# Maxima of attention scores: one head's scores plus the relu of a difference of two heads, in place of copies

## The chip, the cores and the metric

One core of a Trainium2 chip runs the whole program. The metric is the device time of one execution in microseconds (us), as the median of several runs. Names of engines in the views: PE is TensorE (matmuls), PEld its weight loads, ACT is ScalarE, DVE is VectorE, POOL is GpSimd, SP issues the DMAs (SPq is its queue of instructions).

## The reference

The block adds a cross attention and a quantised feed-forward network to x. What bears on this change is the attention, whose softmax is not over the keys: it runs over all heads and batches together, for each pair of a query and a key.

```python
B, S, D, H = (8, 512, 256, 16)        # DK = 16
scores = jnp.einsum('bqhd,bkhd->hbqk', q, k) / np.sqrt(DK)
attn = jax.nn.softmax(scores.reshape(H * B, S, S), axis=0).reshape(H, B, S, S)
out = jnp.einsum('hbqk,bkhd->bqhd', attn, v).reshape(B, S, H * DK)
```

So each of the 512 x 512 pairs needs the maximum of its 128 scores (16 heads x 8 batches) before the exponentials are taken.

## The kernel before, in words

Four stages follow one another, each in a block of its own whose end all engines wait for. `prepare` (0 to 127.6 us) normalises x, projects queries and keys, splits them into bf16 parts and writes these as rows of two stacks in HBM, `k_stack` and `q_stack`; it also makes the values (`vpad`) and the weights of the last stage. `maxima` (127.6 to 310.9 us) finds the maxima. `attend` computes the scores again, exponentials, sums and products with the values. `ffn` is the rest.

`maxima` takes the heads two at a time (a couple p, heads 2p and 2p+1). The queries of both heads lie in one tile `q_both`: one head's 64 rows (4 parts of 16) in partitions 0 to 63, the other's in 64 to 127. The keys of the even head lie in `k_even` with zeros in partitions 64 to 127, those of the odd head in `k_odd` with zeros in 0 to 63, so that a matmul with either tile gives one head's scores. A matmul makes 128 keys (a chunk kc of NC = 4) by 512 queries of one batch, in one bank of PSUM.

The work is cut into 64 groups: a head and two batches (LANES), 4 chunks of keys, so 8 matmuls that fill all eight banks of `ps_max`. Of a group, ACT copies chunks 0 to 2 to SBUF as bf16 (L697, 3 instructions of 1024 elements), DVE takes the larger of `high` and the copies in one instruction (L713, 3072 elements), and takes chunk 3 directly from PSUM (L708, 1024 elements). The order on an engine is the order of the code:

```python
nc.vector.tensor_tensor(high[:, COPIED, :], ps[:, COPIED, :], high[:, COPIED, :], ALU.max)
nc.vector.tensor_tensor(high[:, 0:COPIED, :], copies[:, g % RING], high[:, 0:COPIED, :], ALU.max)
```

At the end L717 folds the two lanes of `high` into `shift`, which `attend` subtracts from the scores (L890).

SP loads the tiles of a couple while the couple before it is worked on (`load_pair`, L109 to L121), then issues three copies of rows inside the stacks that `attend` needs (L64), and at the last couple the first 20 tiles of `attend` (L652, L653). The first couple's even keys and its queries are loaded inside `prepare` (`k_first`, `q_first`, in a piece of the arena `qs` that is free by then), ahead of the last unit's five writes to `q_stack` (L279). POOL ends `prepare` with two memsets: the lower half of `k_first` (L300) and the gaps of `vpad` (L302).

## Time and profile before

| | us |
|---|---|
| runs: median (lowest, highest) of 3 | 859.45 (859.14, 860.92) |
| the profiled execution: its own time | 859.72 |
| its span, first to last instruction | 857.6 |
| of it `maxima`, from L676's first start to the start of `attend` | 127.71 to 310.88 |

The profiled execution's time is its span and 2.1 us around it. Busy times in a view are unions: two instructions of an engine that overlap by their pipelines count once, so the mean of one times their number may be more than the busy time.

### The profile page before, as it was taken

To read this page: it belongs to the slowest core of one execution; us is meant where nothing else is said; L and a number is where in the kernel's file an instruction comes from. 1 tells how busy PE (TensorE), PEld (TensorE's weight loads), DVE (VectorE), ACT (ScalarE), POOL (GpSimd) and SP (SyncE) were. 2 spreads that over 40 slices of the span, in tenths; PEclk is the share of its full clock that TensorE was granted. 3 is DMA by queue.
4 is the path that set the end of the run, shared out by engine and by line. 5 is a ranking of instruction groups with operands and counts; after the bars stand their busy time and mean duration, and the time that the engine had idled before them with its cause. 6 is when DMAs were issued, how large, how long until landed. Compare 5 with 4: busy or idle time off the path is not lost. (4 is left out here: it accounts for less than half of the span.)

```text
span 857.6 us, 20062 instructions
## 1 busy us (share of the span) xinstructions
PE 745.7 (87%) x8150; PEld 448.8 (52%) x8150; DVE 757.3 (88%) x830; ACT 680.7 (79%) x1095; POOL 475.2 (55%) x225
## 2 busy tenths in 40 slices
PE   8898987777777768999999999999999899569977
PEld 6564461112212235767767666767667677425334
DVE  4799638999999979999999999999999995748957
ACT  3444549999999977988999899999999835759873
POOL 1233554000000013999999999999999996414500
PEclk9999999999999989999999999999999999879989
DMA  9897787766776635668867786768867793000014
GB/s 292 275 306 221 245 257 196 196 172 171 196 196 173 245 92 187 185 199 271 258 188 210 242 284 191 227 205 278 253 192 208 223 321 107 0 1 1 1 49 148
DMA packets 98154, 164.30 MB, mean 192 GB/s; under 512 B 9680, under 2 KB 37072, under 8 KB 97744
## 3 DMA queue, kind: packets, MB, share of 16 engines
q1 hardware_dynamic: 98064, 163.03, 63.3%
q8 instruction: 65, 1.06, 0.5%
q14 instruction: 25, 0.20, 0.1%
HBM read 133.63 MB, written 41.94 MB: 205 GB/s over the span
## 5 line engine op out<-in xcount | busy, mean ns | idle before, releaser
L1009 POOL TENSOR_TENSOR e<-e,recip 128x1792 f32<-128x1792 f32 (+3 forms) x128 | 368.1, 2913 | 25.8 <-DVE recip L1040 25.7
L961 ACT ACTIVATE e<-psY 128x512 f32<-128x512 f32 x512 | 296.1, 645 | 41.9 <-PE psY L894 39.0
L1027 DVE TENSOR_REDUCE partial<-e 128x128 f32<-128x2048 f32 (+1 forms) x85 | 284.2, 3360 | 11.8 <-ACT e L961 11.6
L894 PE MATMUL psY<-arena 128*128 128x128 bf16 x2048 | 200.5, 221 | 0.1
L894 PEld LDWEIGHTS psY<-arena 128*128 128x128 bf16 x2048 | 149.0, 98 | 73.8 <-issue 26.6
L697 ACT ACTIVATE copies<-ps_max 128x1024 bf16<-128x1024 f32 x189 | 175.6, 1090 | 0.0
L890 PE MATMUL psY<-shift,minus 128*128 128x512 bf16 x395 | 152.4, 386 | 11.8 <-PEq L633 5.5
L713 DVE TENSOR_TENSOR high<-copies,high 128x3072 bf16<-128x3072 bf16 x63 | 110.3, 1750 | 0.4 <-ACT copies L697 0.4
L1000 POOL MEMSET ones_w<- 96x128 bf16 x1 | 0.2, 206 | 172.6 <-POOLq L633 172.6
L910 PE MATMUL psX<-e,arena 128*32 128x128 f32 x2048 | 76.6, 290 | 2.6 <-DVE e L1020 2.6
L708 DVE TENSOR_TENSOR high<-ps_max,high 128x1024 bf16<-128x1024 f32 x63 | 76.8, 1219 | 1.5 <-PE ps_max L676 1.5
L1020 DVE TENSOR_TENSOR e<-e,psY 128x256 f32<-128x256 f32 (+3 forms) x128 | 76.4, 637 | 1.6
L296 POOL TENSOR_TENSOR parts<-rest,parts 128x512 bf16<-128x512 f32 x32 | 37.7, 1183 | 70.8 <-ACT parts L440 70.7
L967 ACT ACTIVATE psY<-shift 128x512 f32<-128x512 bf16 x117 | 74.2, 634 | 0.0
L910 PEld LDWEIGHTS psX<-e,arena 128*32 128x32 f32 x2048 | 58.5, 110 | 10.8 <-POOL e L1009 2.9
L890 PEld LDWEIGHTS psY<-shift,minus 128*128 128x128 bf16 x395 | 38.6, 98 | 25.0 <-DMA arena<-k_stack 8.0
L910 PE MATMUL acc_last<-e,arena 128*32 128x128 f32 x1024 | 38.2, 288 | 8.2 <-POOL e L1009 7.8
L676 PE MATMUL ps_max<-q_both,k_odd 128*128 128x512 bf16 x128 | 34.5, 382 | 10.9 <-DVE high L708 5.5
L676 PE MATMUL ps_max<-q_both,k_even 128*128 128x512 bf16 x128 | 34.2, 382 | 11.1 <-ACT copies L697 5.7
L676 PE MATMUL ps_max<-arena,k_odd 128*128 128x512 bf16 x128 | 34.0, 382 | 11.1 <-ACT copies L697 5.8
L676 PE MATMUL ps_max<-arena 128*128 128x512 bf16 x128 | 34.0, 382 | 10.8 <-ACT copies L697 4.7
L1434 POOL TENSOR_TENSOR arena<-up,sil 128x512 f32<-128x512 f32 x20 | 25.4, 1270 | 31.8 <-ACT up L1367 24.5
(173 smaller groups left out, 1015.9 us busy)
## 6 DMA issues: line engine op xcount, KB each, us to landing
arena<-k_stack SPq DMA_DIRECT2D x256, 256.0 KB, 3.3
arena<-q_stack SPq DMA_DIRECT2D x64, 256.0 KB, 4.2
k_stack<-parts SPq DMA_DIRECT2D x40, 256.0 KB, 3.7
q_stack<-parts SPq DMA_DIRECT2D x40, 256.0 KB, 3.6
arena<-in_x_dram SPq DMA_DIRECT2D x8, 1024.0 KB, 10.2
k_stack<-k_stack SPq DMA_DIRECT2D x12, 512.0 KB, 11.5
arena<-in_ctx_dram SPq DMA_DIRECT2D x4, 1024.0 KB, 6.5
arena<-q_stack SPq DMA_DIRECT2D x8, 512.0 KB, 8.0
```

The source lines that it names most:

```text
L676: last = nc.tensor.matmul(ps[:, kc, j * S:(j + 1) * S], k_head[:, kc, b * P:(b + 1) * P], q_both[p % 2].rearrange("p c (b q) -> p c b q", ...
L697: nc.scalar.activation(dst, ps[:, kc, :], ACT.Copy).then_inc(copied, 1)
L708: nc.vector.tensor_tensor(high[:, COPIED, :], ps[:, COPIED, :], high[:, COPIED, :], ALU.max).then_inc(direct, 1)
L713: nc.vector.tensor_tensor(high[:, 0:COPIED, :], copies[:, g % RING], high[:, 0:COPIED, :], ALU.max).then_inc(updated, 1)
L890: nc.tensor.matmul(bank[:], minus[:], shift_at(qc, kc).to_broadcast([P, HB, P]), start=True, stop=False, skip_group_check=True)
L894: last = nc.tensor.matmul(bank[:, j * P:(j + 1) * P], ks[:, i % KRING, b * P:(b + 1) * P], qs[:, h, b * P:(b + 1) * P], start=False, stop= ...
L910: last = nc.tensor.matmul(acc[pair // BANK_PAIRS][grp:grp + 32, col:col + P], vpad[:, kc, b, v_col:v_col + 32], e_at(p, z, z + 1), start=F ...
L961: nc.scalar.activation(e_at(p, half * HB, (half + 1) * HB).rearrange("p q z i -> p z q i"), ps[n % SCORES][:].rearrange("p (z q i) -> p z ...
L967: nc.scalar.activation(ps[(n - 1) % SCORES][:].rearrange("p (b q) -> p b q", q=P), shift_at((p + 1) // CHUNK, (p + 1) % CHUNK // PAIRS).to ...
L1009: nc.gpsimd.tensor_tensor(part, part, by_pairs(recip[:, r % 2, :], share), ALU.mult).then_inc(pool_scaled, 1)
L1020: nc.vector.tensor_tensor(part, part, by_pairs(recip_v[:, (r % 2) * P:(r % 2 + 1) * P], BLOCKS - share), ALU.mult).then_inc(dve_scaled, 1)
L1027: nc.vector.tensor_reduce(partial[:, :, k, :], e[:, t:t + n].rearrange("p t q z i -> p q i t z"), AX.XY, ALU.add).then_inc(sum_done, 1)
```

## The change

For key chunks 0 to 2 the larger of two heads' scores is made before any merging, as odd + relu(even - odd). A group is now both heads of a couple and one batch; there are again 64.

- The tile `k_mix` takes the place of `k_even`: even keys in partitions 0 to 63 and, for chunks 0 to 2, the odd head's keys times -1 in 64 to 127. A matmul with it gives even minus odd. POOL makes the negated half from `k_odd` after its load (TENSOR_SCALAR, 64 x 3072, once a couple). Chunk 3 of that half stays zero.
- TensorE, per group: `differences` (3 matmuls to `ps_x`), `plain` (2 matmuls of chunk 3, one a head, to `ps_c`), and for the group before it `larger`: per chunk one matmul of the odd keys and one of the identity `plus` with `gain`, added in the same bank of `ps_y`. 11 in place of 8.
- ScalarE, per group: relu of `ps_x` to `gain` as bf16 (1024 and 512 elements) and a copy of `ps_c` (1024).
- VectorE, per group: the larger of `ps_y` and `shift` (512 and 1024 elements, from PSUM) and of the copies and `high` (1024, bf16 in SBUF). The fold at the end has only chunk 3.
- The odd keys of the first couple are now loaded in `prepare` too, ahead of the other three loads; POOL zeroes their half and makes the first negated half there, ahead of the memset of `vpad`.

```diff
-    if even is not None:
-        sp.dma_start(even[0:HALF], rows(k_stack, 2 * p)).then_inc(loaded, 16)
-    if both is not None:
-        for j in range(2):
-            sp.dma_start(both[j * HALF:(j + 1) * HALF], rows(q_stack, 2 * p + j)).then_inc(loaded, 16)
-    if odd is not None:
-        sp.dma_start(odd[HALF:P], rows(k_stack, 2 * p + 1)).then_inc(loaded, 16)
+    sp.dma_start(odd[HALF:P], rows(k_stack, 2 * p + 1)).then_inc(odd_loaded, 16)
+    sp.dma_start(mix[0:HALF], rows(k_stack, 2 * p)).then_inc(loaded, 16)
+    for j in range(2):
+        sp.dma_start(both[j * HALF:(j + 1) * HALF], rows(q_stack, 2 * p + j)).then_inc(loaded, 16)
...
-                pool.memset(keep["k_first"][HALF:P], 0.0).then_inc(s["k_zeroed"], 1)
-                pool.wait_ge(s["k_zeroed"], 1)
+                pool.memset(keep["k_first"][HALF:P, NC - 1, :], 0.0).then_inc(s["k_zeroed"], 1)
+                pool.memset(keep["k_odd_first"][0:HALF], 0.0).then_inc(s["k_zeroed"], 1)
+                pool.wait_ge(s["k_zeroed"], 2)
+                pool.wait_ge(keep["odd_first_loaded"], 16)
+                nc.gpsimd.tensor_scalar(keep["k_first"][HALF:P, 0:NC - 1, :], keep["k_odd_first"][HALF:P, 0:NC - 1, :],
+                                        -1.0, None, ALU.mult).then_inc(keep["first_negated"], 1)
+                pool.wait_ge(keep["first_negated"], 1)
...
+                def differences(g):
+                    p = g // B
+                    if g % B == 0:
+                        pe.wait_ge(couple_loaded[p % 2], 16 * 3 * (p // 2 + 1))
+                        pe.wait_ge(negated[p % 2], p // 2 + 1)
...
+                    for kc in range(MIXED):
+                        if g:
+                            pe.wait_ge(gained, 2 * (g - 1) + (2 if kc == MIXED - 1 else 1))
+                        nc.tensor.matmul(ps_x[:, kc, :], keys(k_mix, g, kc), queries(g), start=True, stop=True
+                                         ).then_inc(x_scored, 1)
+                def plain(g):
+                    if g:
+                        pe.wait_ge(c_copied, g)
+                    for j, tile in enumerate((k_mix, k_odd)):
+                        last = nc.tensor.matmul(ps_c[:, j, :], keys(tile, g, MIXED), queries(g), start=True, stop=True)
+                    last.then_inc(c_scored, 1)
+                def larger(g):
...
+                    for kc in range(MIXED):
+                        if g:
+                            pe.wait_ge(y_merged, 2 * (g - 1) + (1 if kc == 0 else 2))
+                        nc.tensor.matmul(ps_y[:, kc, :], keys(k_odd, g, kc), queries(g), start=True, stop=False)
+                        pe.wait_ge(gained, 2 * g + (2 if kc == MIXED - 1 else 1))
+                        nc.tensor.matmul(ps_y[:, kc, :], plus[:], gain[:, g % RING, kc, :], start=False, stop=True
+                                         ).then_inc(y_scored, 1)
+                for g in range(GROUPS):
+                    differences(g)
+                    plain(g)
+                    if g:
+                        larger(g - 1)
+                larger(GROUPS - 1)
...
+                for g in range(GROUPS):
+                    if g >= RING:
+                        act.wait_ge(y_scored, MIXED * (g - RING + 1))
+                    for k0, k1 in ((0, MIXED - 1), (MIXED - 1, MIXED)):
+                        act.wait_ge(x_scored, MIXED * g + k1)
+                        nc.scalar.activation(gain[:, g % RING, k0:k1, :], ps_x[:, k0:k1, :], ACT.Relu
+                                             ).then_inc(gained, 1)
+                    act.wait_ge(c_scored, g + 1)
+                    if g > RING:
+                        act.wait_ge(c_merged, g - RING)
+                    nc.scalar.activation(copies[:, g % RING, :] if g else high[:], ps_c[:].rearrange("p j q -> p (j q)"),
+                                         ACT.Copy).then_inc(c_copied, 1)
...
+                for g in range(GROUPS):
+                    for n, (k0, k1) in enumerate(((0, 1), (1, MIXED))):
+                        dve.wait_ge(y_scored, MIXED * g + k1)
+                        if g:
+                            dve.wait_ge(y_merged, 2 * (g - 1) + n + 1)
+                            nc.vector.tensor_tensor(shift[:, k0:k1, :], ps_y[:, k0:k1, :], shift[:, k0:k1, :], ALU.max
+                                                    ).then_inc(y_merged, 1)
...
+                    if g:
+                        dve.wait_ge(c_copied, g + 1)
+                        if g > 1:
+                            dve.wait_ge(c_merged, g - 1)
+                        nc.vector.tensor_tensor(high[:], copies[:, g % RING, :], high[:], ALU.max).then_inc(c_merged, 1)
```

TensorE in the middle of `maxima`, a group before:

```order
L676 MATMUL ps_max<-arena 128x512 [waits max_copied]
L676 MATMUL ps_max<-arena 128x512
L676 MATMUL ps_max<-arena 128x512 [waits max_copied]
L676 MATMUL ps_max<-arena 128x512
L676 MATMUL ps_max<-arena 128x512 [waits max_copied]
L676 MATMUL ps_max<-arena 128x512
L676 MATMUL ps_max<-arena 128x512 [waits max_direct]
L676 MATMUL ps_max<-arena 128x512
```

and a group now (`ps_x` differences, `ps_c` plain scores of chunk 3, `ps_y` the larger ones of the group before):

```order
L680 MATMUL ps_x<-arena 128x512 [waits max_gained] x3
L688 MATMUL ps_c<-arena 128x512 [waits max_c_copied]
L688 MATMUL ps_c<-arena 128x512
L698 MATMUL ps_y<-arena 128x512 [waits max_y_merged]
L700 MATMUL ps_y<-gain,plus 128x512 [waits max_gained]
L698 MATMUL ps_y<-arena 128x512 [waits max_y_merged]
L700 MATMUL ps_y<-gain,plus 128x512 [waits max_gained]
L698 MATMUL ps_y<-arena 128x512 [waits max_y_merged]
L700 MATMUL ps_y<-gain,plus 128x512 [waits max_gained]
```

The two plain matmuls stand between the differences of a group and the six matmuls of the group before it, so TensorE passes to those six only when ScalarE has copied the last `ps_c`.

POOL at the end of `prepare`, before:

```order
L296 TENSOR_TENSOR parts<-rest,parts 128x512 [waits part2_ready] x32
L300 MEMSET arena 64x4096 [waits part3_ready,transposed]
L302 MEMSET arena 128x256x16 [waits k_zeroed]
L229 UNCONDITIONAL_BRANCH
```

and now:

```order
L293 TENSOR_TENSOR parts<-rest,parts 128x512 [waits part2_ready] x32
L297 MEMSET arena 64x1024 [waits part3_ready,transposed]
L298 MEMSET arena 64x4096
L301 TENSOR_SCALAR arena<-arena 64x3072 [waits odd_first_loaded,k_zeroed]
L304 MEMSET arena 128x256x16 [waits first_negated]
L226 UNCONDITIONAL_BRANCH
```

The memset of `vpad` (the last row but one) is now queued behind a load and a multiplication.

SP's only change of order ahead of `maxima` is one more load (the odd keys) in front of the first couple's other three; the last five writes to `q_stack` follow them as before.

## Rows read from the trace of the kernel before

**Rows 1.** The page: the span
```profile
span 857.6 us, 20062 instructions
```

**Rows 2.** Busy time by stretch: PE, PEld, DVE, ACT, POOL (busy us, instructions, granted clock, DMA share, GB/s)
```profile
150.00:200.00 50.00, 38.84 (x145) 9.60 (x144) 50.00 (x36) 50.00 (x55) 0.00 (x0) 1.00 0.69 180
```

**Rows 3.** Groups by line in the stretch 125 to 311 us
```profile
L697 ACT ACTIVATE copies<-ps_max 128x1024 bf16<-128x1024 f32 x189 | 175.6, 1090 | 0.0
...
L713 DVE TENSOR_TENSOR high<-copies,high 128x3072 bf16<-128x3072 bf16 x63 | 110.3, 1750 | 0.4 <-ACT copies L697 0.4
...
L708 DVE TENSOR_TENSOR high<-ps_max,high 128x1024 bf16<-128x1024 f32 x63 | 76.8, 1219 | 1.5 <-PE ps_max L676 1.5
```

**Rows 4.** Timeline inside the stage (start, us, instruction, idle before and releaser)
```profile
198.39 1.75 DVE L713 TENSOR_TENSOR high<-copies,high 128x3072 bf16<-128x3072 bf16 x1
...
198.53 1.47 PE L676 MATMUL ps_max<-q_both,k_even 128*128 128x512 bf16 x6 [0.45 <-DVE high L708]
...
200.05 1.22 DVE L708 TENSOR_TENSOR high<-ps_max,high 128x1024 bf16<-128x1024 f32 x1
...
201.19 1.75 DVE L713 TENSOR_TENSOR high<-copies,high 128x3072 bf16<-128x3072 bf16 x1
```

**Rows 5.** Timeline, the stage's first instructions
```profile
127.71 2.32 PE L676 MATMUL ps_max<-arena 128*128 128x512 bf16 x10 [0.72 <-PEq L229]
...
128.34 2.85 ACT L697 ACTIVATE high<-ps_max 128x1024 bf16<-128x1024 f32 x3 [0.93 <-PE ps_max L676]
```

**Rows 6.** Timeline, a run of 512-column activations of the next stage
```profile
312.12 0.61 ACT L961 ACTIVATE e<-psY 128x512 f32<-128x512 f32 x1 [3.98 <-PE psY L894]
...
314.59 10.70 ACT L961 ACTIVATE e<-psY 128x512 f32<-128x512 f32 x21 [0.16 <-PE psY L894]
```

**Rows 7.** Tile ps_max, durations min/median/max of a matmul
```profile
L676 PE MATMUL ps_max<-q_both,k_even x128: 376/379/391, 148.8 to 294.0; 128*128 128x512 bf16 x128
```

**Rows 8.** Timeline, end of the stage and start of the next
```profile
309.37 1.22 DVE L717 TENSOR_TENSOR shift<-high 128x2048 bf16<-128x2048 bf16 x1
...
310.88 0.21 POOL L1000 MEMSET ones_w<- 96x128 bf16 x1 [172.57 <-POOLq L633]
```

**Rows 9.** Timeline, end of the preparing stage
```profile
111.78 3.51 POOL L300 MEMSET arena<- 64x4096 bf16 x1
...
113.78 0.63 SPq L116 DMA_DIRECT2D arena<-k_stack  x1
...
115.35 3.52 POOL L302 MEMSET arena<- 128x4096 f32 x1
...
115.88 3.31 SPq L279 DMA_DIRECT2D q_stack<-parts  x5
...
127.03 0.38 ACT L483 ACTIVATE wd_row<-psT 128x256 f32<-128x256 f32 x1 [0.86 <-PE psT L407]
```

**Rows 10.** SP's own waits, and the load of 113.78 us to its landing
```profile
SPq L229 <- DMA q_stack<-parts: 7.9, 1, 7.9
...
arena<-k_stack SPq DMA_DIRECT2D x1, 512.0 KB, 5.9
```

**Rows 11.** Busy time by stretch, around the stage's two ends
```profile
110.00:112.00 2.00, 2.00 (x6) 1.62 (x6) 0.25 (x1) 0.79 (x3) 1.87 (x3) 0.50 0.97 299
...
118.00:120.00 2.00, 2.00 (x14) 1.70 (x13) 0.75 (x3) 0.65 (x3) 0.86 (x1) 1.00 1.07 207
...
298.00:301.00 3.00, 2.07 (x8) 0.57 (x8) 3.00 (x4) 3.00 (x5) 0.00 (x0) 1.00 0.18 67
```

**Rows 12.** Groups by line of POOL
```profile
L296 POOL TENSOR_TENSOR parts<-rest,parts 128x512 bf16<-128x512 f32 x32 | 37.7, 1183 | 70.8 <-ACT parts L440 70.7
...
L992 POOL CAST bo_parts<-arena 96x256 bf16<-96x256 f32 x1 | 0.4, 393 | 2.8 <-DMA arena<-in_L_xattn_bo_dram 2.8
```

**Rows 13.** Tile k_odd, issue to landing; timeline of SP at the stage's end
```profile
DMA to landing us min/median/max: 5.6/10.3/11.9
...
283.23 0.35 SPq L652 DMA_DIRECT2D arena<-k_stack  x1
```

More of the change, by code:

```diff
@@ L602, in maxima @@
 def maxima(nc, sem, k_stack, q_stack, keep):
[L611 to L614 removed]
+    shift, plus = keep["shift"], keep["plus"]
     RING = 2
[L616 removed]
+    MIXED = NC - 1
     COUPLES = H // 2
+    GROUPS = COUPLES * B
     with ExitStack() as es:
@@ L620, in head_tile @@
             return es.enter_context(nc.sbuf_tensor(name, [P, NC, CT], BF16))
-        k_even = [keep["k_first"], head_tile("k_even1")]
-        k_odd = [head_tile("k_odd0"), head_tile("k_odd1")]
+        k_mix = [keep["k_first"], head_tile("k_mix1")]
+        k_odd = [keep["k_odd_first"], head_tile("k_odd1")]
         q_both = [keep["q_first"], head_tile("q_both1")]
-        copies = es.enter_context(nc.sbuf_tensor("copies", [P, RING, COPIED, LANES * S], BF16))
+        gain = es.enter_context(nc.sbuf_tensor("gain", [P, RING, MIXED, S], BF16))
+        copies = es.enter_context(nc.sbuf_tensor("copies", [P, RING, 2 * S], BF16))
+        high = es.enter_context(nc.sbuf_tensor("high", [P, 2 * S], BF16))
         spare = es.enter_context(nc.sbuf_tensor("spare_exp", [P, 1], F32))
-        high = es.enter_context(nc.sbuf_tensor("high", [P, NC, LANES * S], BF16))
-        ps = es.enter_context(nc.psum_tensor("ps_max", [P, NC, LANES * S], F32))
-        even_loaded, odd_loaded = ([sem(f"{n}{i}") for i in range(2)] for n in ("even_loaded", "odd_loaded"))
-        scored, copied, direct, updated, tiles_zeroed, folded = (
-            sem(n) for n in ("max_scored", "max_copied", "max_direct", "max_updated", "tiles_zeroed", "max_folded"))
+        ps_x = es.enter_context(nc.psum_tensor("ps_x", [P, MIXED, S], F32))
+        ps_y = es.enter_context(nc.psum_tensor("ps_y", [P, MIXED, S], F32))
+        ps_c = es.enter_context(nc.psum_tensor("ps_c", [P, 2, S], F32))
+        odd_loaded, couple_loaded, negated = ([s, sem(n)] for s, n in (
+            (keep["odd_first_loaded"], "odd_loaded1"), (keep["first_loaded"], "couple_loaded1"),
+            (keep["first_negated"], "negated1")))
+        x_scored, c_scored, y_scored, gained, c_copied, y_merged, c_merged, tiles_zeroed, folded = (
+            sem("max_" + n) for n in ("x_scored", "c_scored", "y_scored", "gained", "c_copied", "y_merged", "c_merged",
+                                      "tiles_zeroed", "folded"))
         with nc.Block() as block:
@@ L635, in _ @@
             def _(sp):
[L636 removed]
+                for p in range(1, COUPLES):
                     if p >= 2:
[L638 to L644 removed]
+                        sp.wait_ge(y_scored, MIXED * B * (p - 1))
+                    load_couple(sp, p, k_stack, q_stack, k_mix[p % 2], k_odd[p % 2], q_both[p % 2],
+                                odd_loaded[p % 2], couple_loaded[p % 2])
+                    for what in STACK_COPIES[COPIES_A_COUPLE * (p - 1):COPIES_A_COUPLE * p]:
+                        copy_rows(sp, k_stack, q_stack, what, keep["k_copied"], keep["q_copied"])
+                for what in STACK_COPIES[COPIES_A_COUPLE * (COUPLES - 1):]:
+                    copy_rows(sp, k_stack, q_stack, what, keep["k_copied"], keep["q_copied"])
                 for c in range(NC):
@@ new lines, in queries, with keys @@
+                def queries(g):
+                    return q_both[g // B % 2].rearrange("p c (b q) -> p c b q", q=P)[:, :, g % B, :]
+                def keys(tile, g, kc, rows=slice(0, P)):
+                    return tile[g // B % 2][rows, kc, g % B * P:(g % B + 1) * P]
+                def differences(g):
[3 more added lines that the diff above has]
+                        pe.wait_ge(negated[p % 2], p // 2 + 1)
+                    if p == 1 and g % B == 0:
+                        pe.wait_ge(tiles_zeroed, 2)
+                    for kc in range(MIXED):
[3 more added lines that the diff above has]
+                                         ).then_inc(x_scored, 1)
@@ L681, in _ @@
+                for g in range(GROUPS):
[4 more added lines that the diff above has]
+                larger(GROUPS - 1)
             @block.gpsimd
             def _(pool):
-                zeros = (k_odd[0], slice(0, HALF)), (k_even[1], slice(HALF, P)), (k_odd[1], slice(0, HALF))
-                for n, (tile, rows) in enumerate(zeros):
-                    if n:
-                        pool.wait_ge(tiles_zeroed, n)
-                    pool.memset(tile[rows], 0.0).then_inc(tiles_zeroed, 1)
+                pool.memset(k_mix[1][HALF:P, MIXED, :], 0.0).then_inc(tiles_zeroed, 1)
@@ new lines, in _ @@
+                pool.memset(k_odd[1][0:HALF], 0.0).then_inc(tiles_zeroed, 1)
+                pool.wait_ge(tiles_zeroed, 2)
+                for p in range(1, COUPLES):
+                    pool.wait_ge(odd_loaded[p % 2], 16 * (p // 2 + 1))
+                    nc.gpsimd.tensor_scalar(k_mix[p % 2][HALF:P, 0:MIXED, :], k_odd[p % 2][HALF:P, 0:MIXED, :],
+                                            -1.0, None, ALU.mult).then_inc(negated[p % 2], 1)
+                    pool.wait_ge(negated[p % 2], p // 2 + 1)
```

83 lines of the change are left out of this document (17 added, 66 removed).

## The prediction

> **What bounds the kernel now.** The page gives the span, 857.6 us [rows 1]; the stage of the maxima is 183 us of it, from the first matmul at 127.71 [rows 5] to the next stage's start at 310.88 [rows 8]. The busy time by stretch comes next: in the middle of the stage DVE and ACT are busy all the time, PE for 38.84 of 50 us, at a granted clock of 1.00 [rows 2]. The groups by line tell which of the two is the limit: DVE's two instructions hardly ever wait (0.4 and 1.5 us in the whole stage) [rows 3]. In the timeline L713 begins at 198.39 and again at 201.19, so a group takes **2.80 us**: 1.66 us from L713 to L708, 1.14 from L708 to L713 [rows 4]. DVE is the bound. ACT is close behind: from (2.85 - 1.02) / 2, a 1024-element copy begins 0.915 us after the one before it [rows 5], so three take 2.75. PE begins a 512-column matmul every (2.32 - 0.38) / 9 = 0.216 us [rows 5, 7]: eight take 1.73. A change pays here if DVE and ACT both get less to do and PE's slack pays for it; 64 groups make each 0.1 us of a group worth 6.4 us.
>
> **Work per group after the change.** DVE's start-to-start times are 1.14 us for 1024 elements from PSUM and 1.66 for 3072 in SBUF [rows 4]. If the fixed part is the same in both, at twice the rate per element in the second (1.66 = f + 1536 u, 1.14 = f + 1024 u), then u = 1.02 ns and f = 0.10 us. The merge of 512 elements from PSUM is then 0.62, that of 1024 from PSUM 1.14, that of 1024 in SBUF 0.62: **2.38** at most; with the 0.60 that a u of 1.04 gives it is 2.34. ACT: two of 1024 at 0.915, and one of 512 at (10.70 - 0.61) / 20 = 0.505 [rows 5, 6], **2.34**. I take relu at the price of a copy of the same size; no relu is in these rows. PE: 11 x 0.216 = **2.38**. All three engines would be full within two per cent, so the handing over decides.
>
> **The ring.** ps_x, ps_c and ps_y fill PSUM once, without a second buffer, and PE works in program order. The longest way round passes through PE and ACT and takes two groups: plain matmuls of group g (2 x 0.216), six of the group before (6 x 0.216), first two differences of g+1 until they can be read (0.216 + 0.379 [rows 7] + 0.04 until ACT begins: the second matmul of a pair begins 0.216 after 127.71 and ACT at 128.34 [rows 5]), then ACT's relu 0.915, small relu 0.505 and the whole of the copy, 1.02, and 0.05 until PE begins the plain matmuls of g+2. 0.432 + 1.296 + 0.635 + 0.915 + 0.505 + 1.02 + 0.05 = 4.85 us, 2.43 a group. DVE's ring is shorter: last merge from PSUM 1.22, 0.05, four matmuls 0.65 + 0.38 + 0.04, in all 2.34. I take **2.43**.
>
> The whole stage: the first plain matmul starts after three differences (0.65), the 64th 63 x 2.43 = 153.1 later; then 0.43 for it and its partner and 0.43 for the first chunk of group 62, 1.07 for its other two, DVE's merge of them 1.27, four matmuls of group 63 1.07, and on DVE 1.14 + 0.62 and a fold of 512 elements to its end 0.69 (0.62, and the 0.08 by which 1.22 is above 1.14): 160.5 us from the first matmul to the end of the fold. Before, this was 309.37 + 1.22 - 127.71 = 182.9 [rows 5, 8]. **-22.4 us.**
>
> **The end of the preparing stage.** Two engines close it nearly together: ACT with L483 at 127.41 [rows 9], and SP, whose last writes to q_stack, issued until 119.2, land 7.9 us after it began to wait, at 127.1 [rows 9, 10]. The new load of odd keys, 512 KB, goes into the same queue ahead of these writes, when the DMA engines are full (share 1.07 at 118 to 120, 207 GB/s) and move up to 300 GB/s elsewhere [rows 11]: it pushes the writes back by 1.7 to 2.5 us. I take 2.0: SP ends at 129.1, ACT's 127.4 is no longer the last, **+1.7 us**. POOL's chain: memsets at 3.51 us for 4096 elements [rows 9], so 0.9 and 3.5 from 111.8 to 116.2; the odd keys, issued at 113.78 like the load that landed in 5.9 [rows 9, 10], are there at 119.7; the multiplication of 3072 elements is priced between a memset (2.6 us) and a two-input instruction (1183 ns for 512, 7.1 us) [rows 9, 12]; nearest is the cast, one input, 393 ns for 256 [rows 12], of which some 0.1 us is fixed: 3.5. Then the vpad memset, 3.52: POOL ends at 126.8, between 125.8 and 130.4. I take it as hidden under SP's 129.1; it costs up to 1.3 us at its upper end.
>
> **What is hidden.** The seven later multiplications (3.5 us each) and the loads of a couple have 7 groups' time, 17 us, since loads are released one group into the couple before; keys land in at most 11.9 us [rows 13], and 11.9 + 3.5 is below 17. If they came late it would be by under 2 us a couple even at 7.1. The next stage's 20 first tiles are issued from 283.23 and over by 298 [rows 11, 13], 15 us; they will be released some 20 us ahead of the stage's end and stay hidden by 5. The matmuls beyond eight a group are in the ring above.
>
> **Sum.** 859.72 (the profiled execution: span 857.6 and 2.1 around it) - 22.4 + 1.7 = 839.0. That execution is 0.3 above the median of the runs, so **838.7 us** against 859.45.
>
> **A rule against it.** While the chip grants the stage a clock of 1.00, PE is idle in short pieces for 22% of it [rows 2]; so short pauses between groups have not lowered the clock. The Trainium skill (TensorE: Matmul & The Clock Gate, "A second HAM failure mode: psum-queue depth-cycling") says that a kernel which goes round the PSUM banks with such small idle pieces sees its clock swing between the two levels. This trace disagrees with it, with its 1.00 over 50 us; by the rule the time would be that of rival 4.
>
> **Rivals.**
> 1. *The handing over costs more.* Engines full to 96 or 98% have nothing to catch up with: each step that comes 0.05 us late in a ring of some six steps adds 0.15 a group. At 2.6 us a group the saving is 11 us less: 850. For it: the three prices are equal within two per cent, and relu and the identity matmuls are in no row. Against: instructions of a kind hardly vary here (376 to 391 ns [rows 7]). 0.17.
> 2. *The start is later.* POOL's chain or the load takes its upper price, and PE, idle for 2.4 us and more before the stage, starts at the lower clock: PE got 0.50 after such a pause at 110 to 112 [rows 11], and some 3 us of it would cost half of that. +2 to +4: 842. 0.10.
> 3. **Slower than before**: *PE stands still behind ps_c.* The plain matmuls of a group wait for ACT's copy of the last one, which ACT does after both relus. If ACT is late, relus and matmuls no longer overlap but take turns: three differences until readable 0.85, two relus and copy to the end 2.44, two handovers 0.1 make 3.4 a group, 64 x 0.97 = 62 us more than in the sum: 901. It decides from 2.75 us a group on, where 64 groups and the later start reach the old 182.9. Against it: while ACT copies, PE has six other matmuls that wait for nothing of that group, and the two-group ring above closes at 2.43. 0.03.
> 4. **Slower**: *the clock falls in the stage.* At the lower level, 1.2 GHz, a matmul takes 0.43, a group 4.75: 64 x 2.32 = 148 us more, 987; already a seventh of the stage at it takes the gain away. Against it: PE will be busier than in the stretch that had 1.00 [rows 2]. 0.03.
> 5. *POOL holds DVE up.* The merge in SBUF has two inputs there, and POOL multiplies beside it for 7 x 3.5 = 25 us; if that quarter of DVE's work stood still as long, 6 us: 845. Rows show only memsets beside L713, which has such inputs, and its mean is 1750 all the same [rows 3]. The GPSIMD Engine Reference of the Trainium skill (its table of the engine's properties) says that the two share SBUF interfaces when a DVE instruction has two SBUF inputs; no multiplication here shows it. 0.04.
>
> **How the numbers follow.** The forecast has 0.63: 832 to 846, from a group of 2.38 (PE's and DVE's own work, -3), a start that loses nothing (-2) and a start of the next stage at full clock after a shorter pause of PE (-1.5), to 2.50 (+4.5) and a start at upper prices (+3). To hold the time 8 times in 10 the range takes rivals 1, 2 and 5: **832 to 852**. A measurement can tell about 0.2%, 1.7 us, from no change. Faster by more: forecast, 1, 2 and 5, less what lies beyond 2.70 us a group: 0.91. Within: 0.03. Slower: 0.06.
>
> **What would show it.** Right: in the new timeline a group takes 2.38 to 2.5 us, DVE and ACT at 93% or more and PE above 93% of the stage, with waits of PE for the copy of ps_c among its longest; SP ends the preparing stage at 128.5 to 130; relus 1.02 and 0.61 us, merges 1.22 and 0.69. Wrong: relus or the identity matmul of another price; a granted clock under 1.00 inside the stage; PE waiting for DMA or POOL at the first group of a couple; a group above 2.6 us with no engine full.

## The result and the profile after

The change makes the kernel slower: **890.67 us** (median of 4 runs, 889.51 to 891.96) against 859.3 for the kernel before beside it, a ratio of 1.0376 [1.035, 1.0402]. Forecast were 838.7 us, 832 to 852: wrong in direction and outside the range. The profiled execution took 889.51 us, with a span of 887.6 against 857.6 [rows 1]. The 30.0 us between the spans lie so, by each stage's first matmul:

| us | before | after | forecast | measured |
|---|---|---|---|---|
| `prepare`, until the first matmul of `maxima` | 127.71 | 134.63 | +1.7 | **+6.9** |
| `maxima`, until the first matmul of `attend` | 183.35 | 211.56 | -22.4 | **+28.2** |
| the rest | 546.54 | 541.41 | 0 | -5.1 |

The stage has the loss. Its groups by line (125 to 347 us):

```profile
L744 DVE TENSOR_TENSOR shift<-ps_y,shift 128x1024 bf16<-128x1024 f32 x63 | 77.0, 1223 | 9.8 <-PE ps_y L700 7.5
L752 DVE TENSOR_TENSOR high<-copies,high 128x1024 bf16<-128x1024 bf16 x63 | 76.8, 1218 | 0.0
...
L728 ACT ACTIVATE gain<-ps_x 128x1024 bf16<-128x1024 f32 x64 | 65.5, 1024 | 24.9 <-PE ps_x L680 22.8
...
L744 DVE TENSOR_TENSOR shift<-ps_y,shift 128x512 bf16<-128x512 f32 x63 | 43.1, 684 | 7.0 <-PE ps_y L700 6.0 <-remote 1.0
...
L728 ACT ACTIVATE gain<-ps_x 128x512 bf16<-128x512 f32 x64 | 38.0, 593 | 0.0
L717 POOL TENSOR_SCALAR k_mix<-k_odd 64x3072 bf16<-64x3072 bf16 x4 | 31.8, 7948 | 59.8 <-DMA k_odd<-k_stack 59.8
```

Merges from PSUM (1223, 684 ns) and relus (1024, 593 ns) have the prices of the forecast. Two rows do not: L752, forecast at half the price of a PSUM merge, has a mean of 1218 ns; and POOL's multiplication takes 7948 ns where 3.5 us were taken. The durations of L752 (min/median/max) say that the mean hides two kinds:

```profile
L752 DVE TENSOR_TENSOR high<-copies,high x63: 674/681/6323, 144.7 to 344.6; 128x1024 bf16<-128x1024 bf16 x63
```

56 of them take 0.68 us; seven take 2.44, 5.94, 6.24, 5.84, 5.93, 5.96 and 6.32. Each of the seven begins inside one of POOL's seven multiplications and ends 1.18 us before its record does. One in the timeline:

```profile
165.37 7.95 POOL L717 TENSOR_SCALAR arena<-arena 64x3072 bf16<-64x3072 bf16 x1 [17.04 <-DMA arena<-k_stack]
...
166.19 5.94 DVE L752 TENSOR_TENSOR high<-copies,high 128x1024 bf16<-128x1024 bf16 x1
...
167.23 0.81 PE L680 MATMUL ps_x<-q_both,k_mix 128*128 128x512 bf16 x3
172.06 1.81 DVE L744 TENSOR_TENSOR shift<-ps_y,shift 128x512 bf16<-128x512 f32 x2
172.23 1.02 ACT L733 ACTIVATE copies<-ps_c 128x1024 bf16<-128x1024 f32 x1 [5.17 <-DVE high L752]
173.15 1.51 ACT L728 ACTIVATE gain<-ps_x 128x1024 bf16<-128x1024 f32 x2
```

The merge ends at 172.13, POOL's record at 173.32. In between everybody stands: ACT's copy waits for the tile that the merge reads, PE's plain matmuls wait for ACT's copy. TensorE after it:

```profile
173.31 0.61 PE L688 MATMUL ps_c<-q_both,k_mix 128*128 128x512 bf16 x1 [5.27 <-ACT copies L733]
173.71 0.63 PE L688 MATMUL ps_c<-q_both,k_odd 128*128 128x512 bf16 x1
174.13 0.63 PE L698 MATMUL ps_y<-q_both,k_odd 128*128 128x512 bf16 x1
...
177.96 0.38 PE L688 MATMUL ps_c<-q_both,k_mix 128*128 128x512 bf16 x1
178.18 0.38 PE L688 MATMUL ps_c<-q_both,k_odd 128*128 128x512 bf16 x1
```

For over 4 us a matmul begins every 0.43 us, then every 0.22 again. Busy time by stretch (length, then PE, PEld, DVE, ACT, POOL, granted clock, DMA share, GB/s) has the same: full clock, the stall, the lower level of 1.2 GHz for most of 7 us, full clock.

```profile
160.00:166.00 6.00, 5.99 (x29) 2.32 (x28) 5.75 (x7) 5.78 (x8) 0.63 (x1) 1.00 0.72 169
166.00:172.00 6.00, 1.99 (x9) 0.66 (x8) 6.00 (x2) 1.06 (x2) 6.00 (x1) 0.93 1.30 345
172.00:179.00 7.00, 5.69 (x16) 2.13 (x17) 4.98 (x7) 4.50 (x6) 1.32 (x1) 0.58 0.39 163
179.00:186.00 7.00, 6.99 (x32) 2.72 (x31) 6.67 (x9) 6.79 (x9) 0.00 (x0) 1.00 0.00 1
```

From one L752 to the next, undisturbed groups take 2.38 and 2.56 us in turn, **2.47**; around a multiplication come groups of 7.6, 4.3 and 3.0 us. The first is the stall (5.1 above 2.47), the other two the slow matmuls (2.3).

The end of `prepare`, and how SP waited there:

```profile
122.55 8.00 POOL L301 TENSOR_SCALAR arena<-arena 64x3072 bf16<-64x3072 bf16 x1 [3.38 <-DMA arena<-k_stack]
...
128.29 0.38 ACT L485 ACTIVATE wd_row<-psT 128x256 f32<-128x256 f32 x1 [0.86 <-PE psT L409]
130.61 3.52 POOL L304 MEMSET arena<- 128x4096 f32 x1
134.44 0.61 SPq L115 DMA_DIRECT2D k_odd<-k_stack  x1
```

```profile
SPq L226 <- DMA q_stack<-parts: 9.6, 1, 9.6
...
SPq L226 <- PEq L226: 2.3, 1, 2.3
```

ACT's last copy begins 1.3 us later than before [rows 9]; SP's writes land 3.6 us after that; POOL ends last, at 134.13, and SP stands 2.3 us at the block's end for it. This profile is at the late end of a spread: in seven others with the same `prepare` (from the experiments below) the first matmul of the stage comes at 130.5 to 133.5 us. The `prepare` of the kernel before has it at 127.7, 127.3 and 128.4 in three profiles.

### The profile page after: what moved, and what is told of

Same layout as the page of the kernel before. It is cut to its first block and busy times, and to the rows that moved or that the text cites. A ratio compares the mean times of both kernels' runs of the same rounds, so it can differ in the third digit from the quotient of the medians.

```text
span 887.6 us, 20617 instructions
## 1 busy us (share of the span) xinstructions
PE 780.8 (88%) x8307; PEld 477.8 (54%) x8342; DVE 768.7 (87%) x894; ACT 657.1 (74%) x1095; POOL 533.7 (60%) x233
## 5 line engine op out<-in xcount | busy, mean ns | idle before, releaser
L744 DVE TENSOR_TENSOR shift<-ps_y,shift 128x512 bf16<-128x512 f32 x126 | 118.6, 954 | 16.8 <-PE ps_y L700 13.4
L728 ACT ACTIVATE gain<-ps_x 128x1024 bf16<-128x1024 f32 (+1 forms) x128 | 96.8, 808 | 24.9 <-PE ps_x L680 22.8
L733 ACT ACTIVATE copies<-ps_c 128x1024 bf16<-128x1024 f32 x63 | 64.6, 1025 | 33.3 <-DVE high L752 33.3
L752 DVE TENSOR_TENSOR high<-copies,high 128x1024 bf16<-128x1024 bf16 x63 | 76.8, 1218 | 0.0
L700 PE MATMUL ps_y<-gain,plus 128*128 128x512 bf16 x179 | 72.2, 404 | 0.0
L717 POOL TENSOR_SCALAR k_mix<-k_odd 64x3072 bf16<-64x3072 bf16 x4 | 31.8, 7948 | 59.8 <-DMA k_odd<-k_stack 59.8
L717 POOL TENSOR_SCALAR arena<-arena 64x3072 bf16<-64x3072 bf16 x3 | 23.8, 7946 | 55.4 <-DMA arena<-k_stack 55.4
L345 PE MATMUL psP<-xT,wq_p 128*128 128x512 f32 x64 | 35.8, 692 | 5.7 <-DVE xT L521 3.4
```

The source lines that it names most:

```text
L700: nc.tensor.matmul(ps_y[:, kc, :], plus[:], gain[:, g % RING, kc, :], start=False, stop=True).then_inc(y_scored, 1)
L728: nc.scalar.activation(gain[:, g % RING, k0:k1, :], ps_x[:, k0:k1, :], ACT.Relu).then_inc(gained, 1)
L744: nc.vector.tensor_tensor(shift[:, k0:k1, :], ps_y[:, k0:k1, :], shift[:, k0:k1, :], ALU.max).then_inc(y_merged, 1)
L752: nc.vector.tensor_tensor(high[:], copies[:, g % RING, :], high[:], ALU.max).then_inc(c_merged, 1)
```

## Experiments

The theory from these rows: POOL's multiplication holds up the DVE instruction whose two inputs are both in SBUF, for nearly its whole length, and the stall then costs TensorE its clock. Rivals: the extra load, the clock by itself, some lateness of the key tiles. In the cuts of code, "..." marks lines left out. Every kernel ran beside the kernel before (858 to 859 us); "stage" is from the first matmul to the end of the fold, 182.9 before and 211.1 after.

**Without the seven multiplications.** Left out are POOL's multiplications in `maxima`; the negated keys of couples 1 to 7 are missing and the maxima with them. All loads stay.

```diff
-                        pe.wait_ge(negated[p % 2], p // 2 + 1)
+                        if p == 0:
+                            pe.wait_ge(negated[0], 1)
...
-                pool.memset(k_mix[1][HALF:P, MIXED, :], 0.0).then_inc(tiles_zeroed, 1)
+                pool.memset(k_mix[1][HALF:P], 0.0).then_inc(tiles_zeroed, 1)
...
-                for p in range(1, COUPLES):
...
-                    nc.gpsimd.tensor_scalar(k_mix[p % 2][HALF:P, 0:MIXED, :], k_odd[p % 2][HALF:P, 0:MIXED, :],
-                                            -1.0, None, ALU.mult).then_inc(negated[p % 2], 1)
```

> POOL's seven multiplications of the stage are left out (the negated half of k_mix is zeros or the first couple's, so the maxima are not the reference's); the one in the preparing stage stays. Theory (VectorE's merge with both inputs in SBUF stands still while GpSimd multiplies): every L752 takes 0.68 us, a group 2.47 us throughout, the stage about 163 us from first matmul to the end of the fold in place of 211.1, the clock 1.00 in it, total 890.7 - 48 = 843. Rival A (the stalls come from the loads of the next couple, which land in the same stretch and stay in): L752 still takes 6 us seven times, total 885 or more. Rival B (the clock falls by itself from PE's short pauses): stretches at 0.50 stay, total above 860.

Measured: 842.69 us, ratio 0.9806 [0.9776, 0.9835]. Durations of the SBUF merge, and busy time by stretch:

```profile
L748 DVE TENSOR_TENSOR high<-copies,high x63: 681/681/682, 140.4 to 293.4; 128x1024 bf16<-128x1024 bf16 x63
```

```profile
150.00:200.00 50.00, 49.80 (x224) 19.58 (x222) 48.56 (x62) 48.72 (x61) 0.00 (x0) 1.00 0.67 180
```

No long merge, no low clock, a stage of 163.5 us: 47.6 less than after. The loads are all still there, so they are not the cause.

**VectorE multiplies.** The seven multiplications move to DVE, after the fifth group of the couple before.

```diff
...
+                    if g % B == B - 4 and g // B + 1 < COUPLES:
+                        p = g // B + 1
+                        dve.wait_ge(odd_loaded[p % 2], 16 * (p // 2 + 1))
+                        nc.vector.tensor_scalar(k_mix[p % 2][HALF:P, 0:MIXED, :], k_odd[p % 2][HALF:P, 0:MIXED, :],
+                                                -1.0, None, ALU.mult).then_inc(negated[p % 2], 1)
```

> The seven multiplications of the stage are done by VectorE, between the merges of the fourth and the fifth group of the couple before; the first stays on GpSimd in the preparing stage. Theory: no merge above 0.7 us; a multiplication of 64 x 3072 bf16 takes VectorE about 0.9 us, at most 3.3 at one element a cycle, so the stage is 163 + 7 x 0.9 = 169 us at most, total 845 to 850. Rival (it is the reading and writing of k tiles next to the loads that is slow, whichever engine does it): the multiplication takes several us on VectorE too, total above 870.

Measured: 848.13 us, ratio 0.9865 [0.9819, 0.9912], stage 169.4. The whole work of 7.95 us on POOL takes DVE 0.96:

```profile
170.25 0.96 DVE L751 TENSOR_SCALAR arena<-arena 64x3072 bf16<-64x3072 bf16 x1
```

The result is a complete kernel that is 1.3% faster than before: it pays for the multiplications openly, with seven groups of 3.44 us.

**POOL in six pieces.** The same work on POOL, each multiplication cut into six of 512 columns.

```diff
...
-                    nc.gpsimd.tensor_scalar(k_mix[p % 2][HALF:P, 0:MIXED, :], k_odd[p % 2][HALF:P, 0:MIXED, :],
-                                            -1.0, None, ALU.mult).then_inc(negated[p % 2], 1)
+                    for c in range(MIXED):
+                        for half in range(2):
+                            x = slice(half * CT // 2, (half + 1) * CT // 2)
+                            nc.gpsimd.tensor_scalar(k_mix[p % 2][HALF:P, c, x], k_odd[p % 2][HALF:P, c, x],
+                                                    -1.0, None, ALU.mult).then_inc(negated[p % 2], 1)
...
```

> GpSimd multiplies in six instructions of 64 x 512 in place of one of 64 x 3072. Theory 1 (VectorE waits for the end of the instruction that GpSimd is in): L752 takes at most 0.7 + 1.4 us, and each couple meets two or three such waits of about 1 us: the stage is 165 to 175 us, total 845 to 858. Theory 2 (the port stays with GpSimd over its queued instructions): as the change, L752 of 6 us, total 890.

Measured: 843.24 us, ratio 0.9818 [0.9785, 0.9852], stage 164.4: a little better than the first theory's 845 to 858.

```profile
L721 POOL TENSOR_SCALAR k_mix<-k_odd x24: 1486/1487/1944, 137.0 to 267.0; 64x512 bf16<-64x512 bf16 x24
```

```profile
L756 DVE TENSOR_TENSOR high<-copies,high x63: 675/681/1045, 140.0 to 293.8; 128x1024 bf16<-128x1024 bf16 x63
```

POOL works longer in sum (6 x 1.49 = 8.9 us), yet the longest merge is 1.05 us and no group is over 2.7: nearly all 47 us are back. It is the length of one POOL instruction that costs, not POOL's work in sum.

**POOL in three pieces.** As before, with 1024 columns each.

> GpSimd's multiplication in three instructions of 64 x 1024 (2.75 us each by the slope between 1.49 us for 512 and 7.95 for 3072). Theory (a merge waits for what is left of the instruction that GpSimd is in, up to about 0.5 us for 512 and 6.1 for 3072 from its start, on a line 1.6 for 1024): merges up to 2.2 us, 1 to 2 of them a couple, stage 170 us at most, total 844 to 850. Rival (below some length GpSimd's instructions never hold VectorE, whatever is left of them): as in six, 843.

Measured: 848.43 us, ratio 0.9887 [0.9854, 0.9919], stage 169.7.

```profile
204.06 8.46 POOL L719 TENSOR_SCALAR arena<-arena 64x1024 bf16<-64x1024 bf16 x3 [12.11 <-DMA arena<-k_stack]
...
207.29 1.19 DVE L754 TENSOR_TENSOR high<-copies,high 128x1024 bf16<-128x1024 bf16 x1
```

The price of a piece (2.77 us) and the total came as expected, the longest merge did not: 1.19 us, where 2.2 were expected, and two or three of them a couple. Every merge that is held up ends 1.19 us before the record of the piece (208.48 against 209.67, the end of the second of the three), as in the kernel after (172.13 against 173.32). If it then works for its undisturbed 0.68, it starts to work about 1.87 us before the end of POOL's record. By this a piece of 2.77 us keeps a merge from working for its first 0.9 us, the whole one of 7.95 for 6.1. In the run with six pieces merges end 0.33 us before the record, so they start 1.02 before it: a piece of 1.49 us holds a merge for its first 0.47 alone.

**The kernel before, with such a multiplication.** POOL multiplies a tile of its own, which nobody reads, once in each of seven couples.

```diff
...
+                pool.memset(busy[HALF:P], 1.0).then_inc(busied, 1)
+                for p in range(1, COUPLES):
+                    pool.wait_ge(odd_loaded[p % 2], 16 * (p // 2 + 1))
+                    for i in range(1):
+                        pool.wait_ge(busied, 1 * (p - 1) + i + 1)
+                        nc.gpsimd.tensor_scalar(busy[HALF:P], busy[HALF:P], -1.0, None, ALU.mult).then_inc(busied, 1)
```

> The kernel before, with a multiplication of 64 x 3072 bf16 by GpSimd on a tile of its own once in each of seven couples; nothing waits for it. Theory: L713, whose inputs both lie in SBUF, meets each of them once and takes up to 8 us there; L708 keeps 1.22; about 7 x (8 - 1) us less what ScalarE and TensorE catch up (nothing, VectorE is the bound): total 859 + 45 to 55 = 904 to 914. Rival (the stall is of the new kernel's own chain, not of the port): 859, L713 at 1.75 throughout.

Measured: 897.09 us, ratio 1.0446 [1.0412, 1.0479], stage 221.1; 904 to 914 were expected, with 7 us for each meeting, and the long merges are 4.9 to 6.0 us above their usual 1.74.

```profile
L716 DVE TENSOR_TENSOR high<-ps_max,high x63: 1209/1211/1225, 131.9 to 344.2; 128x1024 bf16<-128x1024 f32 x63
L721 DVE TENSOR_TENSOR high<-copies,high x63: 1740/1742/7735, 133.5 to 345.3; 128x3072 bf16<-128x3072 bf16 x63
```

No data, tile or semaphore links the two engines here, and still seven of the SBUF merges take 6.6 to 7.7 us, while no merge from PSUM is touched. Here the stage's 38.2 us are the stalls alone: the seven long merges are 37.9 us over 7 x 1.742. All seven end 0.12 us before POOL's record. With their own 1.74 us of work they start 1.86 before it, as the short merges above do. It goes the other way too: two of the multiplications began while a merge was at work, and it was they that got longer, 8.63 and 9.45 us in place of 7.95:

```profile
194.49 1.74 DVE L721 TENSOR_TENSOR high<-copies,high 128x3072 bf16<-128x3072 bf16 x1
194.59 9.45 POOL L695 TENSOR_SCALAR busy<-busy 64x3072 bf16<-64x3072 bf16 x1 [20.64 <-DMA k_odd<-k_stack]
```

The clock falls here too:

```profile
174.88 1.74 DVE L721 TENSOR_TENSOR high<-copies,high 128x3072 bf16<-128x3072 bf16 x1
175.02 4.58 PE L678 MATMUL ps_max<-q_both,k_odd 128*128 128x512 bf16 x14 [5.54 <-DVE high L716]
...
177.69 1.74 DVE L721 TENSOR_TENSOR high<-copies,high 128x3072 bf16<-128x3072 bf16 x1
```

```profile
174.00:181.00 7.00, 5.57 (x18) 1.86 (x19) 7.00 (x6) 6.71 (x8) 0.00 (x0) 0.74 0.01 2
```

but the group after the stall lasts 2.81 us as always, although the granted clock is 0.74 in this stretch: with eight matmuls a group PE has the slack for it, with eleven it has none.

**The kernel before, with memsets instead.** Three memsets of 64 x 3072 in place of each multiplication (`pool.memset(busy[HALF:P], 1.0)`).

> The kernel before, with three memsets of 64 x 3072 bf16 by GpSimd (2.65 us each, 8 us) where the earlier run had one multiplication, once in each of seven couples. Theory (it is GpSimd's reading of SBUF that keeps VectorE's second input out; a memset reads nothing): L713 stays at 1.75 us, total 859. Rival (any long use of SBUF by GpSimd, writing too, holds VectorE): L713 of several us seven times, total 880 to 897.

Measured: 860.9 us in one run, against 858.08 (855.26 to 862.71) for the kernel before; stage 183.3.

```profile
L721 DVE TENSOR_TENSOR high<-copies,high x63: 1744/1744/1759, 135.1 to 308.7; 128x3072 bf16<-128x3072 bf16 x63
```

```profile
L695 POOL MEMSET busy<- 64x3072 bf16 x21 | 55.7, 2652 | 85.4 <-DMA k_odd<-k_stack 84.6
```

POOL was busy for 55.7 us beside the merges, as in the kernel after, and held up none, though multiplications of nearly the length of one of these memsets (2.77 us, above) did. So the memsets that stood beside L713 before [rows 3] could not have shown the cost. A memset reads nothing, and that the reading makes the difference fits this run; no run shows that it is the reading and no other difference of the two.

**Chunk 3 read from PSUM.** In the kernel after, DVE takes the larger of `ps_c` and `high` directly, first in its group; ACT's copy goes. No DVE instruction of a group then has two SBUF inputs.

```diff
...
-                        pe.wait_ge(c_copied, g)
+                        pe.wait_ge(c_merged, g)
...
+                    dve.wait_ge(c_scored, g + 1)
...
+                        nc.vector.tensor_tensor(high[:], plain_v, high[:], ALU.max).then_inc(c_merged, 1)
...
```

> GpSimd multiplies as in the change, in one instruction; VectorE reads chunk 3 straight from PSUM (one input in SBUF in place of two) and ScalarE does not copy it. Theory (only a VectorE instruction with both tensor inputs in SBUF stands still beside GpSimd's multiplication): no merge above 1.3 us although GpSimd is at work for the same 8 us seven times; VectorE's own work is 1.14 + 0.62 + 1.14 = 2.90 us a group, so 64 x 2.90 + 5 = 190 us of stage, total 866 to 872, and no group beyond 3.1 us. Rival (any VectorE instruction stands still beside GpSimd): merges of 6 us as in the change, total 910 or more.

Measured: 961.06 us, ratio 1.1201 [1.1159, 1.1244]. The total missed by 90 us, through a ring that I had built myself:

```profile
PEld ps_c L688 <- DVE high L739: 126.2, 55, 2.3
PE ps_c L688 <- DVE high L739: 99.1, 55, 1.8
...
DVE shift L746 <- PE ps_y L700: 71.6, 110, 1.1
```

PE's plain matmuls wait for DVE's merge of `ps_c`, and DVE's next merges wait for the matmuls that PE issues behind them. What it was made for came out all the same: with seven POOL multiplications of 7.95 us beside them, no merge got longer; the one that now reads `ps_c` has one length:

```profile
L739 DVE TENSOR_TENSOR high<-ps_c,high x63: 1215/1215/1215, 140.0 to 409.7; 128x1024 bf16<-128x1024 f32 x63
```

PE stood still for 1.8 us in each group of 4.35 here, 62 times, and the granted clock stayed at 1.00.

**Plain matmuls last.** Six pieces, and PE's `larger(g - 1)` ahead of `plain(g)`. It tests the ring through `ps_c` from which 2.43 us a group were forecast.

```diff
...
                     differences(g)
-                    plain(g)
                     if g:
                         larger(g - 1)
+                    plain(g)
...
```

> The run with GpSimd's multiplication in six instructions; TensorE does the six matmuls of the group before ahead of the two plain ones, so that it no longer stands before ScalarE's copy of ps_c with six ready matmuls behind. Theory (the two-group ring through ps_c and ScalarE makes 2.47 us a group, TensorE's own work is 2.38): groups of 2.38, the stage 164.4 - 64 x 0.09 = 158.6 us, total 837 to 838. Rival (TensorE's own work and waiting of any kind make the 2.47): no change, 843; or, if VectorE's ring is now the longer, slower.

Measured: 840.15 us, ratio 0.9792 [0.9758, 0.9825], stage 159.2 where 158.6 were expected, an undisturbed group 2.37 to 2.38.

```profile
150.00:200.00 50.00, 49.97 (x231) 20.90 (x229) 50.00 (x63) 49.55 (x64) 20.15 (x13) 1.00 0.68 180
```

PE, DVE and ACT are full: the ring was the limit, and without it the engines' own work is, 11 x 0.216 = 2.38. The same kernel once more, beside the ones that follow:

> The run with the two plain matmuls last once more, as the measure for the next two on the same chip: 840, stage 159.2 us. Theory and rival expect the same.

838.54 us, ratio 0.977 [0.974, 0.98]. The two profiles of this one kernel differ around the stage: it starts 6.5 us after ACT's last copy in the first and 4.5 in the second, and what follows the stage takes 545.7 and 542.8 us. Differences of 2 or 3 us outside the stage are within this spread.

**The first couple's multiplication on VectorE.** It stands in `prepare`, behind the last but one value tile, once on the kernel in six pieces and once on the one with the plain matmuls last.

```diff
-                nc.gpsimd.tensor_scalar(keep["k_first"][HALF:P, 0:NC - 1, :], keep["k_odd_first"][HALF:P, 0:NC - 1, :],
-                                        -1.0, None, ALU.mult).then_inc(keep["first_negated"], 1)
...
+                    if v == NC * B // 2 - 2:
+                        dve.wait_ge(keep["odd_first_loaded"], 16)
+                        nc.vector.tensor_scalar(keep["k_first"][HALF:P, 0:NC - 1, :],
+                                                keep["k_odd_first"][HALF:P, 0:NC - 1, :],
+                                                -1.0, None, ALU.mult).then_inc(keep["first_negated"], 1)
```

> The run with GpSimd's multiplication in six instructions, and the first couple's multiplication in the preparing stage done by VectorE before its last addition of values. Theory (GpSimd's 8 us and its memset behind them close the preparing stage): the stage begins at SP's arrival, 1.5 to 2.5 us sooner after ScalarE's last copy, total 841 to 842 against 843.2. Rival (the stage's start is set by the landing of q_stack alone): unchanged, 843.

Measured: 844.03 us, ratio 0.9833 [0.9805, 0.9861]; from ACT's last copy to the stage 4.1 us instead of 6.5, yet the total does not differ from the six pieces, which is what the rival expected. SP's wait for POOL at the block's end fell from 2.1 to 0.2 us: POOL no longer closes `prepare`, but no gain in the total is shown.

> The run with the two plain matmuls last, and the first couple's multiplication done by VectorE in the preparing stage. Theory (GpSimd's chain closes the preparing stage 2.3 to 2.4 us after SP's arrival): the stage starts 4.1 us after the start of ScalarE's last copy in place of 6.5, total 2 us less than the run it is compared with, 838. Rival (what is won there is lost in the next stages, whose loads or clock decide): no difference.

Measured: **836.86 us**, ratio 0.974 [0.9707, 0.9774], the lowest of all. The stage starts 4.95 us after ACT's last copy, where 4.1 were expected; without the edit it was 6.5 and 4.5. Against the same kernel without this edit on the same chip (838.54) the 1.7 us lie within the intervals, so a gain is not shown here either.

**The load of the odd keys behind the writes.** On the kernel with plain matmuls last, the first odd load is issued after the last five writes to `q_stack`, and DVE multiplies at the stage's start.

> The run with the two plain matmuls last, the first couple's odd keys loaded behind the last writes to q_stack in place of ahead of them, and multiplied by VectorE at the stage's very start. Theory (the load ahead of the writes delays SP's arrival by 3.5 to 4.5 us): SP arrives about when it did before the change, within 1 us of ScalarE's last copy, the first difference waits for load and multiplication instead, 2 to 3 us into the stage: total 1 to 2 us below the run with VectorE's multiplication in the preparing stage, 836 to 837. Rival (the load costs the same wherever it stands): equal to that run.

Measured: 840.29 us, ratio 0.9783 [0.9754, 0.9813]; 836 to 837 were expected. SP now arrives 1.4 us after ACT's last copy began, against 2.2 to 4.8 in the other kernels of the change. From the last issue of the writes to their landing it is 8.2 us, against 9.6 to 10.2 with the load ahead (7.9 in the kernel before [rows 10]): the load does push the writes back. But what was gained is lost at once:

```profile
130.58 3.50 POOL L714 MEMSET k_odd<- 64x4096 bf16 x1
...
131.28 3.62 DVE L744 TENSOR_SCALAR arena<-arena 64x3072 bf16<-64x3072 bf16 x1 [4.36 <-DMA arena<-k_stack]
```

The multiplication that takes DVE 0.96 us elsewhere takes 3.62 here, beside a POOL memset, and ends 0.82 us after it; the first matmul waits for the multiplication.

## Why the prediction was wrong

**Right.** The prices per instruction: matmuls every 0.216 us, relu at the price of a copy (1.02 and 0.59), merges of 1.22 and 0.68. The ring through `ps_c`: 2.43 forecast, 2.47 measured in undisturbed groups, and gone (2.38) once the plain matmuls came last. Without the seven multiplications the stage took 163.5 us; 160.5 were forecast, and 64 x 0.04 = 2.6 of the difference is what a group took beyond 2.43. The loads of a couple and the first tiles of the next stage stayed hidden. Rivals 1 and 3 did not come about. While the stage runs undisturbed, with short waits of PE for `ps_c`, the clock stays at the 1.00 of the stretches above. Inside the stage it fell in six of the seven stalls, in which PE stood still for 5.0 to 5.5 us. The rule of the Trainium skill that was weighed (TensorE: Matmul & The Clock Gate, "A second HAM failure mode: psum-queue depth-cycling") was not borne out by these stretches.

**The step that failed** is the one under "What is hidden", on the seven later multiplications of POOL. They did come in time, each done 9.0 to 11.5 us before the first matmul that needs it, but what they do to others was put at nothing in the sum. Rival 5 named this mechanism and got 6 us and a chance of 0.04; it cost 47.6 us. The Trainium skill's GPSIMD Engine Reference (Specifications, the table of the engine's properties) says that GpSimd shares its SBUF interfaces with VectorE, and that they contend when the VectorE instruction has two SBUF inputs or works in a mode that uses two ports. The runs with multiplications agree (0.68 us became up to 6.32, 1.74 up to 7.74). The run with memsets shows that it is not so for every instruction of GpSimd, and whether the VectorE multiplication that took 3.62 us beside a memset was in such a mode no view shows. In the prediction three things about this term were wrong:

1. The multiplication takes 7.95 us, not 3.5, and more than the upper bound of 7.1. I took the cast of 256 elements as the nearest row; the two-input instruction (1183 ns for 512) would have been nearer.
2. "If that quarter of DVE's work stood still as long": it is not a share. Merges come every 2.47 us, so one meets every multiplication, and once it does it waits for nearly all that is left of it. In sum the L752 take 76.8 - 63 x 0.681 = 33.9 us too much.
3. The clock was a rival of its own (rival 4), not a follower of this one. PE stands for 5.0 to 5.5 us, runs at half speed afterwards, and has no slack to hide it: 47.6 - 33.9 = 13.7 us, about the 6 x 2.3 of the slow groups. That they come from the clock is argued from the two traces (0.43 us a matmul, and no such groups in the kernel before with its slack); no run took the clock away alone.

What I took for evidence against it (L713's mean of 1750 beside memsets) was none: memsets of 55.7 us hold up nothing, multiplications of the same sum cost 38 us. The trace of the kernel before did have the cost, in `prepare`, on instructions too short to show in any sum. DVE's L508 has two inputs in SBUF, of 8 elements each; it takes 0.17 us, and 1.14 where POOL's two-input L296 is at work (L506 likewise, 1.06):

```profile
L508 DVE TENSOR_TENSOR rstd<-rstd,tmp x4: 168/168/1137, 14.7 to 77.6; 128x8 f32<-128x8 f32 x4
```

```profile
77.58 1.16 POOL L296 TENSOR_TENSOR parts<-rest,parts 128x512 bf16<-128x512 f32 x1 [0.42 <-ACT parts L440]
77.62 1.14 DVE L508 TENSOR_TENSOR rstd<-rstd,tmp 128x8 f32<-128x8 f32 x1
```

**The end of `prepare`**: +1.7 forecast, +6.9 measured, 5.2 more, where rival 2 had +2 to +4. ACT's last copy comes 1.3 later, which lies within the spread: it begins at 125.8 to 127.0 in three profiles with the `prepare` of before, and at 124.0 to 129.0 in those of the change. SP's writes land 3.6 after it (2.0 forecast for the load); POOL, which I took "as hidden under SP's", ends another 2.3 later, by the same price of 8.0 instead of 3.5 us. The load pushes the writes back by 2.1 to 3.0 us: 0.7 to 1.2 for its own issue ahead of theirs, and the rest in the queue (9.6 to 10.2 us from issue to landing, 8.2 with the load behind them), so the 2.0 of the forecast was a little low. The stage's first 5.8 us do run at the lower clock, as rival 2 said. The row it leaned on was read loosely: before 110 us PE had not one pause of 2.4 us but two of 1.1 with two small matmuls between.

**The sum, mended.** 839.0 by the forecast, +47.6 in the stage for the multiplications, +3.0 for the rest of the stage, +5.2 at the start, -5.1 in the rest of the program: 889.7, measured 889.51. This adds up because the terms are read from the same two profiles. The -5.1 behind the stage stays unexplained; that part has the same instructions, and over all fourteen profiles here it takes from 541.4 (this one) to 547.7 us, and 545.7 and 542.8 in two profiles of one kernel. So both it and a part of the +5.2 at the start may be chance.

## What to carry to other kernels

Work given to an idle engine is free only if it shares nothing: ask which operands its instructions read from SBUF and what the busy engine reads there meanwhile, and look in the whole trace, other stages too, for a row with that very pair of instructions (a memset does not stand for a multiplication). The longest instance of a group against its median shows what its mean hides. Where the two must share, cut the idle engine's instruction into pieces shorter than the busy engine's other work, or give the work to the faster engine: here six pieces turned a kernel that was 3.8% slower into one that is 1.8% faster, and another order on TensorE brought it to 2.1 and 2.3% in two measurements. And when engines are balanced to the last per cent, a stall costs more than its length, since nobody can catch up.

## What the runs showed of the hardware that I had not expected

- GpSimd's bf16 multiplication by a constant takes 1.49 us for 512 elements of a row, 2.77 for 1024 and 7.95 for 3072, so (7.95 - 1.49) / 2560 = 2.5 ns an element; VectorE does the 3072 in 0.96 us.
- A VectorE instruction with both inputs in SBUF that begins inside such a multiplication works only in its last 1.87 us by the record (7.95 and 2.77 us long alike, and for merges of 0.68 and 1.74 us alike), or in its last 1.02 us where it is 1.49 us long. These figures are worked out, as the undisturbed duration and what was left of GpSimd's record. One with an input in PSUM is not touched (1215/1215/1215 ns).
- A multiplication of GpSimd that begins while such a VectorE instruction is at work is the one that gets longer: 8.63 and 9.45 us in place of 7.95.
- A GpSimd memset holds up no two-input merge (1744/1744/1759 ns), but a one-input bf16 multiplication of VectorE took 3.62 us beside one instead of 0.96. That was seen once; why the two differ no run here shows.
- In six stalls, in which TensorE stood still for 5.0 to 5.5 us, the granted clock fell to its lower level and stayed there for 6.8 us each time. In the kernel before with POOL's multiplications it did the same, and the groups behind the stall took their usual 2.81 us all the same.
